# The last stage of a fused transformer block: activations turned by VectorE and SBUF-to-SBUF DMAs in place of TensorE transposes

## The reference

```python
x = x + 0.5 * ffn(layernorm(x))          # 512 -> 64, per-unit 16-wide relu network, 64 -> 512
x = x + attn(layernorm(x))               # delta-rule attention, then:
#   x1 = attention(rmsnorm(x)) + x;  h = rmsnorm(x1);  gelu(h @ w1 + b1) @ w2 + b2 + x1   (512 -> 2048 -> 512)
x = x + 0.5 * ffn(layernorm(x))          # the second FFN, same weights as the first
```

## Time and profile before

| what | value |
|---|---|
| median of 3 runs | 3310.85 us |
| lowest, highest | 3306.76, 3311.95 us |
| profiled execution, span from first to last instruction | 3308.1 us |
| mean granted TensorE clock | 0.983 of full |
| third stage | from about 1770 us to the end |

### The profile page before, as it was taken

How to read it: one execution, slowest core, us unless ns; L and a number is a source line. 1 busy time by engine, 2 the same in 40 slices (tenths; PEclk the granted TensorE clock), 3 DMA queues, 4 the chain that set the end, 5 groups by cost and what they waited for, 6 DMA issues and landing times.

```text
span 3308.1 us, 148527 instructions
## 1 busy us (share of the span) xinstructions
PE 3162.9 (96%) x68236; PEld 2588.3 (78%) x68236; DVE 1828.6 (55%) x2949; ACT 1406.0 (43%) x3166; POOL 1229.9 (37%) x1225
## 2 busy tenths in 40 slices
PE   6999999999958999999999999999999999999998
PEld 4777777777747888889888778887777878777886
DVE  6787878778648888888423333333333324333333
ACT  5444445444413555554543334333333433333433
POOL 1336564655526777766311222202122212122221
PEclk9999999999978999999999999999999999999999
DMA  3445545455465777766751110101110010111010
GB/s 105 149 148 167 141 157 156 149 150 162 139 204 171 218 225 218 219 210 206 213 165 35 39 39 13 39 28 37 39 39 26 26 39 26 39 39 39 13 39 26
DMA packets 390597, 355.09 MB, mean 107 GB/s; under 512 B 58448, under 2 KB 320720, under 8 KB 388304
## 3 DMA queue, kind: packets, MB, share of 16 engines
q1 hardware_dynamic: 388128, 350.87, 34.3%
q10 hardware_dynamic: 2224, 0.90, 0.2%
HBM read 183.93 MB, written 153.09 MB: 102 GB/s over the span
## 4 chain that ended last, share of the span: by engine, by line
PE 61%; DVE 7%; issue 2%; ACT 1%; DMA 0%; SPq 0%; DVEq 0%; ACTq 0%
PE bank L237 14%; PE bank L235 14%; PE bank L236 14%; PE bank L1230 8%; PE bank L1315 6%; DVE tmp L1480 2%; DVE sysf L1484 2%; PE bank L1702 2%; PE bank L1693 2%; PE bank L1685 1%; PE bank L1676 1%; DVE zb L1503 1%; DVE oT_lo L1497 1%; DVE xt L1468 1%; DVE sysf L1459 0%
## 5 line engine op out<-in xcount | busy, mean ns | idle before, releaser
L1943 DVE TENSOR_TENSOR glo<-gl,gh 128x512 fp32r<-128x512 f32 x256 | 196.2, 766 | 822.7 <-ACT gh L1821 820.9
L1817 ACT ACTIVATE gl<-bank,b1m 128x512 f32<-128x512 f32 x256 | 176.6, 690 | 736.6 <-PE bank L237 730.9
L235 PE MATMUL bank<-h,w_hi 128*128 128x512 f32 x1024 | 420.6, 411 | 0.1
L235 PE MATMUL bank<-w_hi,gh 128*128 128x512 f32 x1024 | 402.8, 393 | 0.7 <-DVE glo L1943 0.7
L237 PE MATMUL bank<-h,w_lo 128*128 128x512 f32 x1024 | 400.8, 391 | 0.0
L237 PE MATMUL bank<-w_hi,glo 128*128 128x512 f32 x1024 | 400.3, 391 | 0.0
L236 PE MATMUL bank<-h,w_hi 128*128 128x512 f32 x1024 | 398.8, 389 | 0.0
L236 PE MATMUL bank<-w_lo,gh 128*128 128x512 f32 x1024 | 398.5, 389 | 0.0
L1230 PE MATMUL bank<-ringA 32*32 32x32 f32 x16384 | 344.0, 196 | 9.8 <-issue 6.8
L1230 PEld LDWEIGHTS bank<-ringA 32*32 32x32 f32 x16384 | 271.5, 104 | 8.5 <-issue 4.2
L1384 ACT ACTIVATE de<-bank 128x64 f32<-128x64 f32 x512 | 114.5, 224 | 301.0 <-PE bank L1230 295.6
(11 more groups left out here) (198 smaller groups left out, 7422.4 us busy)
## 6 DMA issues: line engine op xcount, KB each, us to landing
ringB<-heads_scratch SPq DMA_DIRECT2D x256, 192.0 KB, 3.3
ringA<-heads_scratch SPq DMA_DIRECT2D x256, 128.0 KB, 3.0
X<-in_L_attn_x SPq DMA_DIRECT2D x16, 1024.0 KB, 10.0
x_scratch<-X SPq DMA_DIRECT2D x16, 1024.0 KB, 4.5
heads_scratch<-vb SPq DMA_DIRECT2D x16, 1024.0 KB, 5.2
heads_scratch<-qk SPq DMA_DIRECT2D x16, 1024.0 KB, 6.6
heads_scratch<-kb SPq DMA_DIRECT2D x16, 1024.0 KB, 5.2
heads_scratch<-kbuf SPq DMA_DIRECT2D x16, 1024.0 KB, 7.2
```

The lines of the kernel that those rows point to most:

```text
L235: e.matmul(o, lhs[0], rhs[0], start=first, stop=False)
L1817: e.activation(gl[k][:, :], bank[1 - k][:, :], ACT.Gelu_apprx_tanh, bias=b1m[:, m:m + 1]).then_inc(a_gl, 1)
L1943: e.tensor_tensor(gh[k][1][:, :], gl[k][:, :], gh[k][0][:, :], ALU.subtract).then_inc(v_gl, 1)
```

## The change

The transposes of tiles' h (tiles 1 to 15) and x (tiles 0 to 14) leave TensorE. VectorE turns H in 32x32 blocks, four instructions of 128x512, into a new tile HT at m = 11 (h) and m = 3 (x); sixteen DMAs on SP's queue, each of 32 partitions x 4 runs of 512 bytes (64 KB), then move the blocks to the partitions where they belong, in x2T. The tokens of x2T come out in another order; gelu and relu put them back by reading their bank in 32-wide pieces. `x_turned` is gone; `h_turned` and `h_low` read x2T instead of a bank. z of the next tile is now also read into H by a DMA (`load_next`), squared there at m = 8, 9 and scaled in place at m = 11, so that Z is needed by GpSimd alone. g and relu buffers now lie in HT's space. The last tile's halves stay with TensorE.

```diff
+            HT = sbuf(st, "HT", [P, 4 * NF, NB, 32])
+        work3 = HT[:, :, :, :].rearrange("p (w f) b i -> p w (f b i)", w=NB)
+        relu3, g3, junk3 = [work3[:, i, :] for i in range(2)], work3[:, 2, :], work3[:, 3, :]
+        MOVED = 16 * 16
 # sp_dense
             def load_x1(t):
-                e.wait_ge(p_ht3, 4 * t + 4)
-                if t:
-                    e.wait_ge(p_xt3, 4 * t)
+                if t:
+                    e.wait_ge(v_tx, 4 * t)
+                else:
+                    e.wait_ge(p_ht3, 4)
                 e.dma_start(H[:, :, :], x1_v[t]).then_inc(d_H, 16)
+            def load_next(t):
+                e.wait_ge(o_zx, 4 * t)
+                e.dma_start(H[:, :, :], z_v[t]).then_inc(d_zH, 16)
+            def move(landed):
+                for a4 in range(4):
+                    for q in range(4):
+                        e.dma_start(xT3[32 * q:32 * q + 32, :, a4 * P:(a4 + 1) * P],
+                                    HT[32 * a4:32 * a4 + 32, q:4 * NF:4, :, :].rearrange("j f b i -> j f (b i)"),
+                                    ).then_inc(landed, 16)
+            def move_x(t):
+                e.wait_ge(v_tx, 4 * t + 4)
+                e.wait_ge(a_hi3, 4 * t + 8)
+                e.wait_ge(v_lo3, 4 * t + 8)
+                move(d_x3)
+            def move_h(t):
+                e.wait_ge(v_th, 4 * t)
+                if t >= 2:
+                    e.wait_ge(p_win, NT + t - 1)
...
+                move(d_h3)
+            load_x1(0)
...
             for t in range(NT):
-                load_x1(t)
+                if t:
+                    load_x1(t)
+                    move_x(t - 1)
+                if t + 1 < NT:
+                    load_next(t + 1)
                 if t:
                     store(t - 1)
                 if t + 1 < NT:
+                    move_h(t + 1)
                     load_z(t + 1)
 # pe_dense: turn_h and turn_x are gone
             def hidden(t):
-                e.wait_ge(a_xT3, 4 * t + 4)
+                e.wait_ge(d_x3, MOVED * (t + 1))
 # act_dense
             def h_turned(t, f):
-                e.wait_ge(p_ht3, 4 * t + f + 1)
                 if f == 0:
+                    e.wait_ge(d_h3, MOVED * t)
                     e.wait_ge(p_up, NM * t)
-                e.activation(hT3[0][:, f, :], bank[6 + f % 2][:, :], ACT.Copy, scale=ln2[:, f:f + 1]).then_inc(a_hi3, 1)
+                e.activation(hT3[0][:, f, :], xT3[:, f, :], ACT.Copy,
+                             scale=ln2[:, f:f + 1]).then_inc(a_hi3, 1)
-                    if t + 1 < NT and m in (12, 13):
-                        square(t + 1, 2 * (m - 12))
-                        square(t + 1, 2 * (m - 12) + 1)
+                    if t + 1 < NT and m in (8, 9):
+                        square(t + 1, 2 * (m - 8))
+                        square(t + 1, 2 * (m - 8) + 1)
 # dve_dense
+            def turn(b):
+                return e.transpose(HT[:, :, b, :], H[:, b, :])
+            def turn_h(t):
+                if t >= 2:
+                    e.wait_ge(p_wout, 4 * (NT + t - 1))
+                for b in range(NB):
+                    e.wait_ge(v_hs, 4 * t + b + 1)
+                    turn(b).then_inc(v_th, 1)
+            def turn_x(t):
+                if t:
+                    e.wait_ge(d_h3, MOVED * (t + 1))
+                for b in range(NB):
+                    e.wait_ge(a_y3, 4 * t + b + 1)
+                    turn(b).then_inc(v_tx, 1)
+                elif m == 3:
+                    turn_x(t)
-                    if t + 1 < NT and m == 13:
+                    if t + 1 < NT and m == 10:
                         mean_square(t + 1)
-                    if t + 1 < NT and m == 14:
+                    if t + 1 < NT and m == 11:
                         scale_h(t + 1)
+                        turn_h(t + 1)
```

More of the change, by code:

```diff
@@ L1593, in macaron @@
             w2 = sbuf(st, "w2_hi", [P, NM, D], F32R), sbuf(st, "w2_lo", [P, NM, D], F32R)
-            g3 = sbuf(st, "g3", [P, TOK])
+            HT = sbuf(st, "HT", [P, 4 * NF, NB, 32])
             stats3 = sbuf(st, "stats3", [P, NB, 6])
@@ L1598, in macaron @@
             nm3 = sbuf(st, "nm3", [P, NB])
-            relu3 = [sbuf(st, f"relu3{i}", [P, TOK]) for i in range(2)]
+        work3 = HT[:, :, :, :].rearrange("p (w f) b i -> p w (f b i)", w=NB)
+        relu3, g3, junk3 = [work3[:, i, :] for i in range(2)], work3[:, 2, :], work3[:, 3, :]
         stage3 = [xT3[:, f, :] for f in range(NF)] + [Z[1][:, b, :] for b in range(NB)]
@@ L1607, in macaron, with by_block, in_order @@
         HALF, LAST = TOK // 2, NT - 1
+        MOVED = 16 * 16
+        def by_block(v):
+            return v.rearrange("p (a b i) -> p b a i", a=4, b=NB)
+        def in_order(v):
+            return v.rearrange("p (b a i) -> p b a i", a=4, b=NB)
         def half(k):
             return slice(k * HALF, (k + 1) * HALF)
-        d_H, d_w3 = sems("d_H d_w3")
+        d_H, d_w3, d_zH, d_x3, d_h3 = sems("d_H d_w3 d_zH d_x3 d_h3")
         SMALL3 = 16 * 2
@@ L1619, in macaron @@
             "a_whi3 a_ss a_hi3 a_xT3 a_gl a_gh a_y3 a_relu3")
-        v_wlo3, v_ms, v_hs, v_lo3, v_gl, v_x2, v_bn3, v_ag3, v_nm3, v_g3, v_o = sems(
-            "v_wlo3 v_ms v_hs v_lo3 v_gl v_x2 v_bn3 v_ag3 v_nm3 v_g3 v_o")
+        v_wlo3, v_ms, v_hs, v_lo3, v_gl, v_x2, v_bn3, v_ag3, v_nm3, v_g3, v_o, v_tx, v_th = sems(
+            "v_wlo3 v_ms v_hs v_lo3 v_gl v_x2 v_bn3 v_ag3 v_nm3 v_g3 v_o v_tx v_th")
         o_ms, o_zx, o_sb, o_rs3, o_xb3 = sems("o_ms o_zx o_sb o_rs3 o_xb3")
@@ L1635, in load_x1 @@
             def load_x1(t):
-                e.wait_ge(p_ht3, 4 * t + 4)
                 if t:
-                    e.wait_ge(p_xt3, 4 * t)
+                    e.wait_ge(v_tx, 4 * t)
+                else:
+                    e.wait_ge(p_ht3, 4)
                 e.dma_start(H[:, :, :], x1_v[t]).then_inc(d_H, 16)
+            def load_next(t):
[16 more added lines that the diff above has]
+                    e.wait_ge(p_win, NT + t - 1)
+                else:
+                    e.wait_ge(v_wlo3, 12)
+                move(d_h3)
             def store(t):
@@ L1742, in turn_half @@
                     m.then_inc(p_xt3, 1)
-                    released[bk] = a_xT3, 4 * LAST + 2 * k + n + 1
+                    released[bk] = a_xT3, 2 * k + n + 1
             def hidden_half(k):
-                e.wait_ge(a_xT3, 4 * LAST + 2 * k + 2)
+                e.wait_ge(a_xT3, 2 * k + 2)
                 bank_free(k)
@@ L1759, in ffn @@
             def ffn(t, m):
[L1761 to L1764, removed]
+                if m == 5:
                     hidden(t)
@@ L1774, in pe_dense @@
                     up(t, m)
-                    if m == NM - 1 and t + 1 < NT:
-                        turn_h(t + 1, 0)
-                        turn_h(t + 1, 1)
                     if m:
@@ L1781, in pe_dense @@
                         ffn(t - 1, m)
-                if t + 1 < NT:
-                    turn_h(t + 1, 2)
-                    turn_h(t + 1, 3)
                 down(t, NM - 1)
@@ L1795, in square @@
                 if b == 0:
-                    e.wait_ge(d_x[t % 2], 16 * ((NT + t) // 2 + 1))
-                    if t:
[L1798 to L1802, removed]
+                    e.wait_ge(d_zH, 16 * t)
+                    e.wait_ge(v_hs, 4 * t)
+                    if t == 1:
+                        e.wait_ge(done2, 5)
+                else:
+                    e.wait_ge(a_ss, 4 * t + b)
+                e.activation(junk3, H[:, b, :], ACT.Square, accum_out=ss3[:, b:b + 1]).then_inc(a_ss, 1)
             def h_turned(t, f):
-                e.wait_ge(p_ht3, 4 * t + f + 1)
                 if f == 0:
+                    e.wait_ge(d_h3, MOVED * t)
                     e.wait_ge(p_up, NM * t)
-                e.activation(hT3[0][:, f, :], bank[6 + f % 2][:, :], ACT.Copy, scale=ln2[:, f:f + 1]).then_inc(a_hi3, 1)
+                e.activation(hT3[0][:, f, :], xT3[:, f, :], ACT.Copy,
+                             scale=ln2[:, f:f + 1]).then_inc(a_hi3, 1)
             def gelu(t, m):
@@ L1816, in gelu @@
                     e.wait_ge(d_w3, SMALL3)
-                e.activation(gl[k][:, :], bank[1 - k][:, :], ACT.Gelu_apprx_tanh, bias=b1m[:, m:m + 1]).then_inc(a_gl, 1)
+                made, ordered = bank[1 - k][:, :], gl[k][:, :]
+                if t:
+                    made, ordered = by_block(made), in_order(ordered)
+                e.activation(ordered, made, ACT.Gelu_apprx_tanh, bias=b1m[:, m:m + 1]).then_inc(a_gl, 1)
                 e.wait_ge(a_gl, n + 1)
@@ L1825, in normalize @@
                     e.wait_ge(v_nm3, t + 1)
-                    if t + 1 < NT:
-                        e.wait_ge(p_ht3, 4 * (t + 1) + 4)
-                    e.wait_ge(o_zx, 4 * t + 4)
+                    e.wait_ge(v_th, 4 * t + 4)
                 e.activation(H[:, b, :], Z[t % 2][:, b, :], ACT.Identity, bias=nm3[:, b:b + 1],
                              scale=rs3[:, b:b + 1]).then_inc(a_y3, 1)
```

(24 more changed lines are left out.)

## The result

The change made the kernel slower: 3334.3 us (median of 4 runs, 3332.2 to 3338.0) against 3308.87 us of the kernel before on the same chip, a ratio of 1.0077 with a 95% interval of 1.0066 to 1.0089. The forecast was 3290 us in 3262 to 3347, a gain: the time lies inside the range, but on the wrong side of no change. What came is rival 1, the wait that trips the clock.

The account below looks back on a forecast made before the run. The prediction took TensorE's instruction stream to bound the third stage. Transposes removed (-52.2 us) plus new waits for x (+31.5) gave -20.7, so 3287.4 us of span; with 2.75 us to the median, 3290 us, range 3262 to 3347.

Parts of the forecast that it names:

- rival 1: At the wait of `hidden` for x: a wait near 3.6 us drops TensorE's clock; 3344 us, chance 0.32.
- What bounds the kernel: Third stage: TensorE's stream sets the time, so removing its transposes takes 52 us off the path.
- When x is ready: x path before `hidden`: turns, first move at T + 5.2, 16 issues, landing 2.3 us; complete at T + 15.75.
- T: In each tile of the third stage, the end of `up(t, 3)`, where ScalarE's gelu starts; times are counted from it.
- the issue spacing: SP's 16 moves of x: one issue every 0.55 us, bounds 0.48 and 0.65.
- S: Wait of TensorE's `hidden` for x: 2.1 us a tile, bounds 0.45 and 4.4, 31.5 us over 15 tiles.
- a toll: On SP's queue: whether an SBUF-source DMA lengthens the issue behind it, 0.62 us against 0.48 back to back; left open.
- the clock's point of decision: Wait of `hidden`: the clock falls from some S between 2.3 and 3.6 us, a fall costing 2.1 us.
- The halved rate: Moves to and from 32 partitions at half rate: S of 4 to 4.7 us; chance 0.12 within the 0.32 of rival 1.
- The h path: Turns and moves of h, landed by 17 us after up 11, wanted at 23.1: 6 us of slack, costed at nothing.
- the squares, GpSimd, `load_z`: Side work off TensorE in the tile: 5 us or more of slack for the squares, each costed at nothing.
- The transposes: TensorE's four pieces a tile of 0.87 us, 3.48 us, leave the path: 52 us over 15 tiles.

Follow-up runs that it names:

- experiment 1: Changed kernel with x turned by VectorE one step sooner (m == 2 in place of 3): 3254.35 us, ratio 0.9831 to the kernel before.
- experiment 2: Changed kernel with the load of x1 issued behind the 16 moves of x instead of ahead: 3323.17 us, ratio 1.0048 to the kernel before.
- experiment 5: Changed kernel with the last 2 of the 16 moves of x left out: 3299.31 us, ratio 0.9975 to the kernel before.
- experiment 6: Changed kernel with the last of the 16 moves of x left out: 3315.59 us, ratio 1.0023 to the kernel before.
- experiment 3: Changed kernel with the moves of x cut into 32 of 32 KB, same bytes: 3484.0 us, ratio 1.0534 to the kernel before.
- experiment 9: Changed kernel with x's moves split over SP's and ScalarE's queues and the x1 load behind SP's 8: 3331.58 us, ratio 1.0066 to the kernel before.
- experiment 7: Changed kernel with 8 of the 16 moves of x issued by ScalarE, 8 by SP: 3285.5 us, ratio 0.9937 to the kernel before.
- experiment 8: Changed kernel with 4 DMAs of 128 partitions in place of x's 16 moves, partition permutation left out: 3266.52 us in one execution.
- experiment 4: Changed kernel with x turned by TensorE again, only h by VectorE and DMAs: 3280.12 us, ratio 0.9918 to the kernel before.

## Why the prediction was wrong

- **What bounds the kernel**: right. TensorE's stream is the stage, and 52 us of transposes on it are worth 52 us when nothing is put in their place (experiment 1: -53.7).
- **When x is ready**: the turns (2.48 us for four) and the first issue (T + 5.0) were right, the landing behind the last issue was 2.1 us against 2.3.
- **The step that failed first is the issue spacing**: "I take 0.55", with bounds of 0.48 and 0.65. It is 0.64. The last issue is 15 x 0.09 = 1.4 us later by it; the first issue and the landing took 0.2 us less each, and S became 3.1 to 3.2 in place of 2.1. Part of it was in the rows: in the earlier trace rows the issue of the SBUF-to-SBUF DMA and the one behind it take 0.47 and 0.57, and the prediction asked whether the second was a toll of the first. There is such a toll: the load of x1 takes 0.36 us on its own and 0.59 right behind a move (experiment 2). But a move takes 0.59 even as the first of its run, behind a load, so 0.47 was too low for its own price as well, and no row of before held an issue of its shape.
- **The second step that failed is the clock's point of decision**, "S between 2.3 and 3.6 us" and a price of 2.1. Experiments 2, 5 and 6 showed falls behind waits from 1.9 us on, though not behind all of them, and experiment 2 priced one at 1.65 us. With the forecast's own S near 2 the kernel is not at 3290 but near 3300 (experiment 5: 3299). So even a right S would have given little more than a third of the forecast gain.
- **The halved rate** was not the cause (experiments 1 and 3), and the rate isn't halved. Narrow moves from two queues ran at 203 GB/s with the DMA engines 0.93 busy (the first window of experiment 9), which is about what two queues issue, and at 195 to 251 GB/s with a share of 1.15 to 1.23 in experiment 7; wide ones of the same 512-byte runs in experiment 8 ran at 297 and 274 GB/s with shares of 1.22 and 1.15, the x1 load there at 334. Experiment 8 asked for the busy share per GB/s: that of the wide moves is 0.76 to 0.87 of that of the narrow ones, neither half nor the same. The Trainium skill says in "SBUF — State Buffer", section on the DMA port swizzle, that 32 partitions reach 8 of the 16 ports. This case agrees in direction only. At 203 GB/s the sixteen moves are 5.2 us of data by an estimate, which 10.3 us of issue hide; with two queues and the load's data ahead of them they no longer were hidden (experiment 7).
- **The h path, the squares, GpSimd, `load_z`** at nothing: right. No wait of ScalarE on h is in its list, and experiment 4 gained its 26 us whole.
- **The transposes**, 3.48 us a tile, were sized a little low: 3.67 (experiment 1), 2.8 us over the 15 tiles.
- **Chances**: 0.32 stood on the rival that came. Its price, 3344 us, was 10 us too high, through a fall that costs 1.65 and not 2.1 and a wait of 3.2 to 3.4 and not 3.6.

## What to carry to other kernels

Count DMA issues on a queue as instructions with a duration of their own, and take it from a row in which issues of the same kind stand back to back: here sixteen of 64 KB cost 10.3 us of queue for 5 us of data. When work moves from the bounding engine to a chain turns-issue-landing, place its start by that whole chain; one step sooner turned +25 us into -54 us with one line, with 1.5 us to spare in most tiles and nearly none where one issue of the run was long. A wait that about equals the work it replaces is no draw on TensorE, since the clock can fall behind it.

## What I had not expected of the hardware

- The granted clock fell behind waits of 1.84 to 1.92 us in 5 of 11 tiles, of 2.48 to 2.57 us in 12 of 13, of 2.64 to 2.67 us in 11 of 13, of 3.16 to 3.26 us in 13 of 13; in none of the 13 tiles of experiment 7 with a wait of 1.3 to 1.75 us. A single tile there held the clock behind 2.79 us. TensorE was fully busy before each. The low stretch then held 3.4 us, in a few tiles twice that. Behind the waits of 13 us of experiment 3 it began inside the wait and held 3 to 5 us after TensorE resumed, so those tiles paid for the clock what the others did.
- An issue of 64 KB from SBUF to SBUF takes 0.64 us of its queue, of 32 KB no less by what experiment 3 shows. With two queues SP's stay 0.64 us apart while ScalarE's are 0.65 to 0.66 apart.
- The data of two small moves came behind that of a 1 MB load on another queue, which was issued 0.4 and 1.0 us before them: 5.6 to 5.8 us to land in place of 2.1 (experiment 9).
- In two of 15 tiles of the changed kernel (2 and 9, counted from 1 from the first with `hidden`) one issue takes 1.0 us more than the rest, with a transfer of 16 KB of instructions within 0.3 us of it, and the same two in experiment 2. In experiment 1, where the moves stand elsewhere in time, it is four.
